# Second layer of a four-layer network: a tap's low parts made in eighths between gathers, with loads and high parts of the weights moved

## What is computed

```python
d = conv(conv(x[:, :256], dw_w, dw_b, pad=1, groups=256), pw_w, pw_b)
d = (d - mean(d)) / sqrt(var(d) + eps)             # per image and channel
off = conv(d, off_w, off_b, pad=1)                 # 18 = 9 taps x (y, x)
# for each of the 9 taps: rows of d at four neighbours of a shifted, fractional place
samples = g(y0, x0)*(1-ly)*(1-lx) + g(y0, x0+1)*(1-ly)*lx + g(y0+1, x0)*ly*(1-lx) + g(y0+1, x0+1)*ly*lx
dc = einsum('bckhw,ock->bohw', samples, dc_w) + dc_b
dc = layernorm_over_channels(dc) * ln_g + ln_b
out = x * (d * sigmoid(dc)) + x * g                # g: a gate from max and mean of x[:, 256:]
```

## Time and profile before

| | us |
|---|---|
| median of 3 runs | 4188.23 |
| lowest and highest | 4186.56, 4192.63 |
| the profiled execution's own time | 4190.17 |
| its span, first to last instruction | 4188.4 |

### The profile page before, as it was taken

The page is one execution under the profiler, slowest core; times in us unless marked ns, Lnnn a source line. Parts: engine busy times, 40 slices in busy tenths (PEclk is TensorE's granted clock), DMA queues, the critical chain, the costliest instruction groups (busy, mean ns, idle before and its releaser), DMA issues. The chain is left out here.

```text
span 4188.4 us, 67038 instructions
## 1 busy us (share of the span) xinstructions
PE 3866.5 (92%) x18696; PEld 2423.2 (58%) x18696; DVE 2981.1 (71%) x4504; ACT 2591.7 (62%) x4616; POOL 2088.0 (50%) x1870
## 2 busy tenths in 40 slices
PE   6899999999999999999998999989888467969999
PEld 3555555555555555555556788837667343835553
DVE  7888888888888888888887433376999936245552
ACT  5899999999999999999996433232221431213331
POOL 0555555555555555555552455415777620036663
PEclk8999999999999999999999999999999777979999
DMA  1200000000000000000002000028999911453312
GB/s 49 103 9 12 9 10 9 9 9 9 12 9 10 9 9 9 9 12 9 10 9 87 28 5 1 0 82 340 394 390 397 377 64 62 174 116 71 72 41 81
DMA packets 150518, 326.82 MB, mean 78 GB/s; under 512 B 45785, under 2 KB 50073, under 8 KB 149517
## 3 DMA queue, kind: packets, MB, share of 16 engines
q1 hardware_dynamic: 108940, 174.46, 13.5%
q0 software_dynamic: 41472, 151.01, 9.0%
HBM read 246.14 MB, written 79.04 MB: 78 GB/s over the span
## 5 line engine op out<-in xcount | busy, mean ns | idle before, releaser
L558 POOL TENSOR_TENSOR cpb_sum<-cpb_tab 128x512 f32<-128x512 f32 x1028 | 1046.7, 1051 | 965.0 <-DVE cpb_r L688 964.7
L669 ACT ACTIVATE cpb_h<-cpb_z,net_vec 128x512 f32<-128x512 f32 x1536 | 1007.8, 699 | 50.5 <-PE cpb_z L609 37.8
L606 PE MATMUL cpb_z<-cpb_r,cpb_w2a 128*128 128x512 f32 x2048 | 858.1, 419 | 22.9 <-DVE cpb_h L729 22.9
L688 DVE SCALAR_TENSOR_TENSOR cpb_r<-cpb_sum,cpb_r 128x512 fp32r<-128x512 f32 x1024 | 696.7, 711 | 187.9 <-ACT cpb_r L663 187.9
L607 PE MATMUL cpb_z<-cpb_r,cpb_w2b 128*128 128x512 f32 x2048 | 802.3, 392 | 0.0
L609 PE MATMUL cpb_z<-cpb_r,cpb_w2a 128*128 128x512 f32 x2048 | 800.2, 391 | 0.0
L688 DVE SCALAR_TENSOR_TENSOR cpb_r<-cpb_z,cpb_r 128x512 fp32r<-128x512 f32 x1028 | 662.0, 686 | 160.0 <-ACT cpb_r L663 154.6
L663 ACT ACTIVATE cpb_r<-cpb_z 128x512 fp32r<-128x512 f32 x1028 | 561.1, 604 | 126.6 <-PE cpb_z L593 126.6
L663 ACT ACTIVATE cpb_r<-cpb_sum 128x512 fp32r<-128x512 f32 x1024 | 598.0, 648 | 2.0 <-POOL cpb_sum L558 2.0
L606 PEld LDWEIGHTS cpb_z<-cpb_r,cpb_w2a 128*128 128x128 f32 x2048 | 383.8, 187 | 366.1 <-issue 300.4
L618 PE MATMUL cpb_zo<-cpb_h,cpb_w3w 128*32 128x512 f32 x3584 | 477.3, 605 | 0.0
(11 more groups left out here) (358 smaller groups left out, 5326.5 us busy)
## 6 DMA issues: line engine op xcount, KB each, us to landing
conv_out<-dc_ys SPq DMA_DIRECT2D x576, 64.0 KB, 6.1
cpb_log<-log_dram SPq DMA_DIRECT2D x66, 256.0 KB, 3.2
qk_parts<-gn_r SPq DMA_DIRECT2D x64, 256.0 KB, 2.0
dc_wr<-in_dc_wT SPq DMA_DIRECT2D x9, 1024.0 KB, 5.9
bias_dram<-cpb_bst SPq DMA_DIRECT2D x520, 8.0 KB
net_x<-in_x SPq DMA_DIRECT2D x8, 1024.0 KB, 11.1
sa_qa<-qk_parts SPq DMA_DIRECT2D x16, 512.0 KB
sa_ka<-qk_parts SPq DMA_DIRECT2D x16, 512.0 KB
```

The costliest lines, as they stand in the source:

```text
L558: pool.tensor_tensor(SUM[:, r, :].rearrange("p (y x) -> p y x", x=W), TAB[:, slot, r, 0, :].unsqueeze(1).broadcast_to([P, NF // W, W]), TA ...
L606: pe.matmul(z2[:, bank, :], W2A[:], R1[:, k, :], start=True, stop=False)
L669: act.activation(H2[:, t % 8, :], z2[:, t % 3, :], ACT.Relu, bias=V("cpb_b2")).then_inc(h2a, 1)
L688: v.scalar_tensor_tensor(R2[:, t % RING, :], first_layer(t), 0.0, R1[:, t % RING, :].bitcast(F32), ALU.max, ALU.subtract).then_inc(r2_read ...
```

## The change

The low parts of a tap are made in eighths of 256 columns, one after each chunk's gathers of image 1 of the tap two before. For taps 0 and 1 the eight follow each other. The semaphore `wl_ready` counts eighths, and those who wait for it wait for 8 a tap (9 taps: 72). SyncE loads the weights of tap t from 3 on at chunk 0 of (t-1, 0), one tap later; the load of tap 2 stays. ScalarE casts tap t from 3 on after chunk 4 of (t-1, 0), and tap 2 after chunk 0 of (1, 0).

```diff
-        CHUNKS = HW // P
+        CHUNKS = EIGHTHS = HW // P
...
-                    sp.wait_ge(wl_ready, tap)
+                    sp.wait_ge(wl_ready, EIGHTHS * tap)
...
-                    if b == (tap == 0) and c == 0 and tap < TAPS - 2:
-                        weights(tap + 2)
+
+                    if (tap, b, c) == (0, 1, 0):
+                        weights(2)
+                    elif 2 <= tap < TAPS - 1 and (b, c) == (0, 0):
+                        weights(tap + 1)
...
-            def weights_low(tap):
-
-                pool.wait_ge(wh_ready, tap + 1)
-                if tap >= 2:
-                    pool.wait_ge(y_mm, tap_tiles(tap - 2))
-                pool.tensor_tensor(WL[:, tap % 2], WR[:], WH[:, tap % 2].bitcast(F32), ALU.subtract).then_inc(wl_ready, 1)
-
-            weights_low(0)
-            weights_low(1)
+            def weights_low(tap, e):
+
+                if e == 0:
+                    pool.wait_ge(wh_ready, tap + 1)
+                    if tap >= 2:
+                        pool.wait_ge(y_mm, tap_tiles(tap - 2))
+                k, of = e // 2, slice(e % 2 * C // 2, (e % 2 + 1) * C // 2)
+                pool.tensor_tensor(WL[:, tap % 2, k, of], WR[:, k, of], WH[:, tap % 2, k, of].bitcast(F32), ALU.subtract
+                                   ).then_inc(wl_ready, 1)
+
+            for tap in range(2):
+                for e in range(EIGHTHS):
+                    weights_low(tap, e)
...
-                if b == 0 and tap + 2 < TAPS:
-                    weights_low(tap + 2)
-
+
+                    if b == 1 and tap + 2 < TAPS:
+                        weights_low(tap + 2, c)
...
-                pe.wait_ge(wl_ready, tap + 1)
+                pe.wait_ge(wl_ready, EIGHTHS * (tap + 1))
...
-                        act.wait_ge(wl_ready, TAPS)
+                        act.wait_ge(wl_ready, EIGHTHS * TAPS)
...
-                if b == 1 and tap + 2 < TAPS:
-                    weights_high(tap + 2)
+                    if (tap, b, c) == (1, 0, 0):
+                        weights_high(2)
+                    elif 2 <= tap < TAPS - 1 and (b, c) == (0, 4):
+                        weights_high(tap + 1)
```

## The result

| | us |
|---|---|
| changed kernel, median of 16 runs | 4201.71 (4196.95 to 4204.25) |
| kernel before on the same chip, median of 14 runs | 4190.7 |
| ratio, middle of its 95% interval and the interval | 1.0027 (1.0020 to 1.0035) |
| profiled execution of the changed kernel: time, span | 4198.3, 4196.5 |

Two further executions of the kernel before (5565 and 16615 us) and one of the kernel without low parts (5447 us) were in a slow state and are left out of all medians. The change makes the kernel slower by 11.0 us, 0.26%: just over the 0.2% that can be told from no change. The forecast was +3.4 us and 4191.7, with a range of 4182.5 to 4206. The direction of the sum was right, its size was not. Of the 10 us by which 4191.7 was missed, 2.5 are its starting point: it went from 4188.23, the median of three runs.

A forecast was written before the change was run, and what follows sets the result against it. DMA engines and VectorE were taken to bound the loop, tap 8's low parts the end. The loop's 12 us gain was spent there, leaving +3.4 us: 4193.6, less 1.9 to the median, 4191.7; range 4182.5 to 4206.

The forecast's parts named there:

- The end decides: End of second layer's deformable convolution: tap 8's later low parts delay last copy and moments; shifts(0) +3.4 us.
- The 0.6 us for the lower clock: TensorE at tap 8's start: after standing idle 25 us it runs partly at the lower clock, about 0.6 us more.
- Rival 2: End of the stage does not bind: VectorE reaches shifts(0) at 3289, 11 us earlier; 4177 us; chance 0.06.
- The loop gains about 12 us: Gather loop up to tap 8: low parts whole at 3225.2, against last gathers issued by 3237.54 before.
- the chance of 0.64: Forecast case: tap 8's low parts whole between 3216 and 3230, giving -6 to +8 us, counted as the same.
- Rival 1: GpSimd becomes the loop's bound: pairs slip 0.46 to 0.75 us on 56 occasions; 4206 to 4222 us; chance 0.30.
- Rival 3: Loop: dips and DMA waits turn up elsewhere, period still 56; +16.7 us, 4205; chance within rival 1's 0.30.
- That of the DMA engines: Loop bound: 154.1 MB at 413 GB/s takes 373 us from 2847.5; with 4.6 lost, low parts whole at 3225.2.
- That of VectorE: Loop bound: 107 samples of 3.05 us, about 51 eighths, about 1 us of waits; low parts whole 3216 to 3224.
- the dips: DMA rate beside GpSimd's low-part passes, 350 GB/s: taken to vanish with eighths, leaving 413 GB/s.
- At shifts(0): VectorE's request for the deviation at the stage's end: possible at 3303.3 against 3299.97, +3.4 us.
- Costs put at nothing: Moved loads, casts to high parts, first 16 eighths, TensorE in a tap: no cost; at most 2 us a tap otherwise.

The follow-up runs named there:

- first execution: The profiled execution of the changed kernel, no further edit: 4198.3 us; shifts(0) comes 459.8 us after the first sample.
- second execution: The changed kernel run once more for a second trace, no edit: 4197.36 us; shifts(0) comes 451.2 us after the first sample.

## Why the prediction was right or wrong

**The end decides: right, and close in size.** The step from tap 8's low parts to the last copy was put at 70.3 us and took 71.1 (3232.57 to 3303.62) and 69.5; the wait at shifts(0) was put at 14 and was 13.7 and 13.1. TensorE was to stand idle for 25 us and did for 31.3. Both removing this step from the change and adding it alone to the kernel before confirm it. The 0.6 us for the lower clock are not settled: the granted clock was 0.50, the lower level, until the first copy at 3238.17 in the first execution, which came 5.6 us after the low parts, and already 0.79 from 3230.0 to 3232.4 in the second, where the first copy came after 4.5 us, no later than in the kernel before (4.7). Rival 2 (the end does not bind) fell with that.

**The loop gains about 12 us: too much, and this is the term that was mis-sized.** Low parts whole were forecast at 3225.2; they were at 3232.6 and, in the other execution, at 3227.9, the first outside the 3216 to 3230 on which the chance of 0.64 rested. The +11.0 us also lie outside the -6 to +8 that went with it, though inside the range, whose upper end belonged to rivals 1 and 3. Counted from the first sample to the last gather of (6, 1), the loop gains 2.0 and 9.1 us. Two things were mis-sized.

First the start of the comparison: the row I took for the end of the old gathers (3237.54) is the last but one; the last ends at 3238.99. By that the forecast meant a gain of over 14 us, not 12.

Second, and of more weight, the term for waits. Each bound by itself was sound. That of the DMA engines, with the 4.6 us lost in the last image, gives 3225.2, 368 us from the first sample, and the kernel without low parts took 367.8. That of VectorE gave 359 to 367; with the measured pause of 0.66 us an eighth (3.71 - 3.05), for 55 of them (I had counted 51) and 108.5 samples of 3.05, it is 367.2. I took the larger of the two, and 1 us of waits in VectorE's. The changed kernel needs 373 to 380 us, 5 to 12 above the larger bound. Of the 12 in the first execution 7.5 lie before image 3, where executions differ; of the 5 in the second, 0.9. My reading is that where two resources are within 1% of each other, a delay on either is not made up by the other. The run without low parts supports it from VectorE's side; from the side of the DMA engines it is argued, not shown. In a period: 8 x 3.05 + 8 x 3.71 = 54.1 by VectorE, 54.3 by the DMA engines, 54.7 to 54.8 measured, 53.5 forecast. And I let the dips go altogether. Those beside the passes are gone, but shallower ones stand where the copies pause once a tap (320 GB/s from 2965 to 2970). From 2960 to 3190 us the kernel before moves 393 GB/s, the changed one 400 and 404, not 413.

**At shifts(0)** this makes +11.6 and +5.4 us on the span's scale where +3.4 was forecast (3311.5, 3305.3; before 3300.0); the two executions end at +8.1 and +7.2 us, the medians at +11.0. Counted from the first sample it is +16.7 and +8.1. Between +8 and +11 lies the spread of executions (4196.95 to 4204.25), which no experiment resolves further.

**Costs put at nothing: right in effect.** The casts do wait for their load, 3.5 us each on average, which was not foreseen; no low part waits for a cast in the loop:

```profile
ACT net_conv_w L1381 <- DMA dc_wr<-in_dc_wT: 21.1, 6, 5.1
```

**Rival 1, GpSimd as the bound: fell as stated.** It had a pair slip by 0.46 us or more on 56 occasions. The pair and the eighth take 3.71 us, VectorE's samples beside them the same. Eighths 4 us or more apart occur behind the five that take 1.24 us or more (2985.55 to 2989.77, 4.22 us), and once more (3220.32 to 3224.69), in the second execution three times. But the 0.2 us that GpSimd was to have to spare are gone: in the rows from 2941.88 on it waits for no sample, VectorE is busy throughout, and which of the two sets the 3.71 is not shown. Of the rival remain lesser frictions, its last words. The lock rule of the Trainium skill (SBUF — State Buffer, "Who interferes with whom", the single rule) would have each eighth wait out a VectorE operation. The trace agrees for 5 of the 56 eighths (1.24 to 1.28 us in place of 0.75, a wait of about 0.5), in the second execution for 2, and not for the others.

**Rival 3, the change frees nothing** (period 56, 4205): the period is 1.6 us shorter, so not as stated, but the +11.0 lie nearer to its +16.7 than to +3.4. With the old pass in the change the period is 56.3 and the time +21.3 us, 4.6 above what that rival gave.

## What to carry to other kernels

When a step is cut up and spread over later work, look for the last user that needs all of it: here the later time cost nothing that could be measured for six of seven taps, and 17 to 18 us for the seventh. Where two engines are each near their limit, a bound worked out for each alone is a floor and not a forecast: here the stage took 5 to 12 us more than the larger. Removing the stall from one of them altogether, in an experiment, shows how much there is to gain at most. A wait that falls by two thirds (ScalarE's for stores) is worth nothing while another engine sets the pace.

## What the runs showed of the hardware

A subtraction of 256 columns on GpSimd takes 0.745 us, one of 512 1.30, one of 2048 4.50 to 4.65: eight small ones cost 1.4 us more than one large. By the rate of the Trainium skill (GPSIMD Engine Reference, section 3) the estimate was 0.55 us for an eighth. The step from 256 to 512 columns, 0.56 us, agrees with that rate; the whole eighth does not: some 0.19 us come on top in each operation. VectorE is held for 0.57 us by each eighth, for 1.07 by each quarter (352.27 us busy with 27 of them, less 323.4) and for 3.9 to 4.3 by each pass (three kernels), so the hold follows the columns and not the number of operations.

A gather's issue on GpSimd is not of one length. Behind an eighth the first of a pair takes 1.22 or 1.23 us and the second 1.25 or 1.26 in nearly every pair of the changed kernel; where GpSimd had waited for a sample the first often takes 0.94. That is why a pair and an eighth fill 3.71 us. The ends of the issues are not spread evenly: in the first execution 189 of 210 between 2860 and 3230 us come at the start of a VectorE operation or within 0.2 us after it, where about 57 would by chance. So the operations beside them may set their length; that was not tried. Nor was a kernel with fewer bytes to store, which would have moved the DMA engines' bound alone.
